# Joining the last layer norm with the shared expert and the router, and two scans in place of two loops

## What is computed

```python
x = x + _L0_xattn_ref(_layernorm(x), ...)      # cross attention
x = x + _L0_ffn_ref(_layernorm(x), ...)        # Hadamard-rotated FFN
x = x + _L1_xattn_ref(ctx, _layernorm(x), ...) # selective scan, gated by the norm of x
x = x + _L1_ffn_ref(_layernorm(x), ...)        # 16 experts, two per token, and a shared one

def _L1_ffn_ref(x, Wr, bias, Wg, Wu, Wd, sWg, sWu, sWd):
    xt = x.reshape(b * s, h)                   # 2048 tokens of 512
    probs = jax.nn.softmax(xt @ Wr.T + bias)   # 16 experts
    topk_val, topk_idx = jax.lax.top_k(probs, 2)
    w = topk_val / (jnp.sum(topk_val, axis=-1, keepdims=True) + 1e-9)
    ...                                        # y: each token through each expert
    routed = jnp.einsum('tke,tk,teh->th', one_hot(topk_idx, 16), w, y)
    shared = jax.nn.silu(xt @ sWg) * (xt @ sWu) @ sWd
    return (routed + shared).reshape(b, s, h)
```

## Time and profile before

| | us |
|---|---|
| median of 3 runs (2711.42 to 2715.6) | 2714.7 |
| profiled execution | 2715.96 |
| its span, first to last instruction | 2714.2 |
| last norm stage | 43.3 |

### The profile page before, as it was taken

How to read it: one execution, slowest core, us unless ns; L and a number is a source line. 1 busy time by engine, 2 the same in 40 slices (tenths; PEclk the granted TensorE clock), 3 DMA queues, 4 the chain that set the end, 5 groups by cost and what they waited for, 6 DMA issues and landing times. The chain is left out here.

```text
span 2714.2 us, 35174 instructions
## 1 busy us (share of the span) xinstructions
PE 2294.5 (85%) x10784; PEld 1768.1 (65%) x10785; DVE 1860.2 (69%) x3465; ACT 1229.2 (45%) x2129; POOL 1350.1 (50%) x1083
## 2 busy tenths in 40 slices
PE   3799999999999999997856997998988749468980
PEld 2688888888888888885525665665655427356770
DVE  6476777777676767765757999999989766312223
ACT  2354445445444545443655655656555312123430
POOL 0233333333333333331756778988888602577324
PEclk7799999999999999998977999999999958779995
DMA  7522232221223232112467564654554220755317
GB/s 280 218 75 79 86 110 86 109 87 72 82 86 110 86 110 85 63 67 81 139 219 216 177 205 144 213 175 172 180 195 156 61 90 16 250 164 183 120 54 259
DMA packets 136907, 363.57 MB, mean 134 GB/s; under 512 B 21281, under 2 KB 58913, under 8 KB 118561
## 3 DMA queue, kind: packets, MB, share of 16 engines
q1 hardware_dynamic: 123648, 328.36, 35.6%
q0 software_dynamic: 6320, 20.71, 2.4%
q10 hardware_dynamic: 6768, 12.32, 1.2%
HBM read 290.06 MB, written 71.30 MB: 133 GB/s over the span
## 5 line engine op out<-in xcount | busy, mean ns | idle before, releaser
L664 POOL TENSOR_SCALAR att_probs<-att_probs,att_recip 128x512 f32<-128x512 f32 x256 | 181.7, 713 | 563.1 <-DVE att_recip L731 563.1
L1809 POOL TENSOR_TENSOR mix_drive<-mix_du,mix_rows 128x512 f32<-128x512 f32 x256 | 326.6, 1282 | 63.2 <-DMA mix_rows<-bc_d 28.9
L588 ACT ACTIVATE att_probs<-att_s,att_bias,att_rq 128x512 f32<-128x512 f32 x256 | 200.4, 783 | 289.7 <-DVE att_bias L727 289.6
L1862 DVE TENSOR_TENSOR_SCAN mix_state<-mix_state,mix_drive 128x512 f32<-128x512 f32 x256 | 312.8, 1222 | 15.5 <-POOL mix_drive L1809 10.5
L1693 ACT ACTIVATE mix_state<-mix_delta,mix_a 128x512 f32<-128x512 f32 x256 | 176.7, 692 | 276.9 <-DVE mix_drive L1873 237.7
L1794 POOL TENSOR_TENSOR mix_y<-mix_y,mix_drive 128x512 f32<-128x512 f32 x180 | 230.4, 1280 | 78.2 <-DVE mix_drive L1873 78.2
L1602 PE MATMUL mix_down<-mix_wd,mix_hT 128*128 128x512 f32 x512 | 233.9, 600 | 7.5 <-DVE residual_x L1893 7.5
L726 DVE TENSOR_REDUCE att_nmax<-att_s 128x1 f32<-128x512 f32 x256 | 175.2, 684 | 71.7 <-PE att_s L101 64.8
L767 DVE TENSOR_TENSOR att_pT<-att_pt,att_pT 128x512 fp32r<-128x512 f32 x256 | 170.1, 686 | 65.0 <-ACT att_pT L594 61.3
L594 ACT CAST att_pT<-att_pt 128x512 fp32r<-128x512 f32 x256 | 144.0, 592 | 132.8 <-PE att_pt L445 128.5
L99 PE MATMUL att_w<-att_w_qkv,att_cx 128*128 128x256 f32 x512 | 158.6, 310 | 34.2 <-DVE att_w_qkv L713 25.5
(11 more groups left out here) (348 smaller groups left out, 6718.4 us busy)
## 6 DMA issues: line engine op xcount, KB each, us to landing
att_xn<-normT SPq DMA_DIRECT2D x32, 2048.0 KB
mix_gu<-guT SPq DMA_DIRECT2D x64, 1024.0 KB
mix_rows<-bc_d SPq DMA_DIRECT2D x128, 256.0 KB, 5.0
guT<-att_ffnT SPq DMA_DIRECT2D x32, 512.0 KB, 5.7
mix_wd<-wdT SPq DMA_DIRECT2D x16, 1024.0 KB
slots<-exp_y ACTq DMA_DIRECT2D x47, 256.0 KB
normT<-nrm_outT SPq DMA_DIRECT2D x4, 2048.0 KB, 9.3
exp_raw<-in_L_ffn_Wg SPq DMA_DIRECT2D x16, 512.0 KB
```

What stands on the lines that cost most here:

```text
L588: act.activation(probs[:, n, :], ps_s[n % 2][:, :], ACT.Exp, bias=bias[:, n:n + 1], scale=rq[:, n:n + 1], accum_out=sums[:, n:n + 1]).then ...
L664: pool.tensor_scalar(probs[:, n, :], probs[:, n, :], recip[:, n:n + 1], 1.0, ALU.mult, ALU.mult).then_inc(s_pn, 1)
L1809: pool.tensor_tensor(drive[q % RING][:, :], du[i % DUS][:, :], rows[g % ROWS][:, 0, :], ALU.mult).then_inc(s_drive, 1)
L1862: dve.tensor_tensor_scan(h[:, :], h[:, :], drive[q % RING][:, :], 0.0, ALU.mult, ALU.add).then_inc(s_scan, 1)
```

## The change

`stage_norm` keeps only its first use (the diff there takes out branches and is not shown). The last norm moves into the router's stage, now `stage_norm_router`, and is interleaved with the logits and batch 0's gate and up on each engine. The inverse root becomes one power on GpSimd. The transposes use the banks of `rou_y`, the logits the one bank `rou_bank`. TensorE waits at first for ident and wr alone. The two chains of additions become one scan each; for this `chosen`, `pre` and `place` are stored with the expert outside and the tile inside, and the mask `within` restarts the scan at every expert.

```diff
             def _(sp):
-                sp.dma_start(ident_sb[:, :], ident).then_inc(s_in, 16)
-                sp.dma_start(wr[:, :], Wr).then_inc(s_in, 16)
+                sp.dma_start(ident_sb[:, :], ident).then_inc(s_first, 16)
+                sp.dma_start(wr[:, :], Wr).then_inc(s_first, 16)
...
                 for b in range(B):
+                    sp.wait_ge(s_normed, TB * (b + 1))
+                    sp.dma_start(xrows[b * S:(b + 1) * S, :].rearrange("(t p) d -> p t d", p=P),
+                                 normed[b % 2][:, :, :]).then_inc(s_rowsout[b % 2], 16)
+                for b in range(B):
                     sp.wait_ge(s_yadd, TB * (b + 1))
...
             def _(pe):
+                def turn(b):
+                    for t in range(TB):
+                        pe.wait_ge(s_normed, TB * b + t + 1)
+                        if b:
+                            pe.wait_ge(s_lo, TB * (b - 1) + t + 1)
+                        for k in range(KD):
+                            tr = pe.transpose(ps_y[t][:, k * P:(k + 1) * P], normed[b % 2][:, t, k * P:(k + 1) * P],
+                                              ident_sb[:, :])
+                        tr.then_inc(s_tr, 1)
...
+                def route(b):
+                    pe.wait_ge(s_lo, TB * (b + 1))
+                    if b:
+                        pe.wait_ge(s_lcopied, b)
+                    for k in range(KD):
+                        mm = split_product(pe, bank[0:EXPERTS, :], (wrT[:, 0, k, :], wrT[:, 1, k, :]),
+                                           (xT[b][:, 0, k, :], xT[b][:, 1, k, :]), k == 0, k == KD - 1)
+                    mm.then_inc(s_l, 1)
...
-                pe.wait_ge(s_in, 16 * 6)
+                pe.wait_ge(s_first, 16 * 2)
...
+                turn(0)
                 pe.wait_ge(s_wlo, 1)
...
+                route(0)
+                turn(1)
+                gate(0)
+                up(0)
+                route(1)
+                turn(2)
+                gate(1)
+                turn(3)
+                route(2)
+                up(1)
+                route(3)
+                pe.wait_ge(s_lcopied, B)
+                for n in range(N):
+                    b, t = divmod(n, TB)
+                    tr = pe.transpose(ps_l[:, n, :], logitT[:, b, t * P:(t + 1) * P], ident_sb[0:EXPERTS, 0:EXPERTS])
                 tr.then_inc(s_lt, 1)
-                up_gate(0)
+                for j in range(IC, 2 * IC):
+                    gate(j)
+                    up(j)
+                pe.wait_ge(s_in, 16 * 4)
                 pe.wait_ge(s_chosen, 1)
                 pe.matmul(ps_c, ones[:, :], chosen[:, :, :], start=True, stop=True)
                 pe.matmul(ps_r, before_sb[:, :], chosen[:, :, :], start=True, stop=True).then_inc(s_counts, 1)
-                up_gate(1)
                 down(0)
...
             def _(act):
...
+                turned_hi(0)
+                for n in range(3):
+                    weights_hi(n)
+                logits_out(0)
+                turned_hi(1)
+                silu(0)
+                lift(0)
+                logits_out(1)
+                turned_hi(2)
+                silu(1)
+                turned_hi(3)
+                logits_out(2)
+                hi(0)
+                lift(1)
+                logits_out(3)
+                hi(1)
+                act.wait_ge(s_sub, 1)
+                act.activation(ex[:, :, :], logits[:, :, :], ACT.Exp).then_inc(s_ex, 1)
...
             def _(pool):
+                def invert(b):
+                    pool.wait_ge(s_var, b + 1)
+                    pool.tensor_tensor(rstd[:, b, :], var_eps[:, b, :], power[:, :], ALU.pow).then_inc(s_rstd, 1)
...
+                invert(0)
+                invert(1)
+                weights_lo(0)
+                weights_lo(1)
+                invert(2)
+                weights_lo(2)
+                invert(3)
...
             def _(dve):
+                norm_stats(0)
+                normalize(0)
                 dve.wait_ge(s_whi, 1)
                 dve.tensor_tensor(wrT[:, 1, :, :], ps_t, wrT[:, 0, :, :].bitcast(F32), ALU.subtract).then_inc(s_wlo, 1)
+                norm_stats(1)
+                turned_lo(0)
+                normalize(1)
+                norm_stats(2)
+                turned_lo(1)
+                normalize(2)
+                norm_stats(3)
+                turned_lo(2)
+                normalize(3)
...
+                turned_lo(3)
...
-                for n in range(N):
-                    own.after(dve.tensor_tensor(pre[:, n + 1, :], pre[:, n, :], pair[:, 0, n, :], ALU.add))
+                own.after(dve.tensor_tensor_scan(flat(pre), flat(within), flat(ps_c), 0.0, ALU.mult, ALU.add))
...
-                own.after(dve.tensor_copy(ends[:, 0:1], tiles[:, 0:1]))
-                for e in range(1, EXPERTS):
-                    own.after(dve.tensor_tensor(ends[:, e:e + 1], ends[:, e - 1:e], tiles[:, e:e + 1], ALU.add))
+                own.after(dve.tensor_tensor_scan(ends[:, :], ones[:, 0:EXPERTS], tiles[:, :], 0.0, ALU.mult, ALU.add))
...
-                own.after(dve.tensor_tensor(place[:, :, :], pre[:, 0:N, :], ps_r, ALU.add))
-                own.after(dve.tensor_tensor(place[:, :, :], place[:, :, :], repeat(first[:, :]), ALU.add))
+                own.after(dve.tensor_tensor(place[:, :, :], pre[:, :, :], ps_c, ALU.subtract))
+                own.after(dve.tensor_tensor(place[:, :, :], place[:, :, :], ps_r, ALU.add))
+                own.after(dve.tensor_tensor(place[:, :, :], place[:, :, :], spread(first[:, :], N), ALU.add))
```

More of the change, by code:

```diff
@@ L131, in stage_norm @@
         rstd = m.sb("rstd", [P, TB])
-        keep = isinstance(xT, list)
-        outT = xT if keep else [m.sb(f"outT{i}", [P, 2, KD, S], F32R) for i in range(2)]
+        outT = [m.sb(f"outT{i}", [P, 2, KD, S], F32R) for i in range(2)]
         banks = [m.ps(f"bank{t}", [P, KD, P]) for t in range(TB)]
@@ L2014, in stage_shared_router @@
         wr = m.sb("wr", [EXPERTS, DIM])
+        normed = [m.sb(f"normed{i}", [P, TB, DIM]) for i in range(2)]
+        xT = [m.sb(f"xT{b}", [P, 2, KD, S], F32R) for b in range(B)]
+        stats = m.sb("stats", [P, B, TB, 6])
+        meanvar = m.sb("meanvar", [P, B, TB, 2])
+        var_eps = m.sb("var_eps", [P, B, TB])
+        rstd = m.sb("rstd", [P, B, TB])
+        power = m.sb("power", [P, TB])
         wrT = m.sb("wrT", [P, 2, KD, EXPERTS], F32R)
@@ L2094, in _ @@
                                  xs[:, b * TB:(b + 1) * TB, :]).then_inc(s_st, 16)
+                for i in range(2):
+                    sp.wait_ge(s_rowsout[i], 16 * B // 2)
                 sp.wait_ge(s_st, 16 * B)
@@ new lines, in project @@
+                def project(j, which, out, done, free):
+                    b, ic = divmod(j, IC)
+                    cols = slice(ic * P, (ic + 1) * P)
+                    if j == 0:
+                        pe.wait_ge(s_sw, which + 1)
+                    if j:
+                        pe.wait_ge(free, j)
+                    for k in range(KD):
+                        mm = split_product(pe, out[:, :], (part(0, which, k)[:, cols], part(1, which, k)[:, cols]),
+                                           (xT[b][:, 0, k, :], xT[b][:, 1, k, :]), k == 0, k == KD - 1)
+                    mm.then_inc(done, 1)
@@ L2145, in _ @@
                 pe.matmul(ps_r, before_sb[:, :], chosen[:, :, :], start=True, stop=True).then_inc(s_counts, 1)
-                up_gate(1)
                 down(0)
-                up_gate(2)
+                for j in range(2 * IC, 3 * IC):
+                    gate(j)
+                    up(j)
                 for n in range(2 * N):
@@ L2153, in _ @@
                 down(1)
-                up_gate(3)
+                for j in range(3 * IC, 4 * IC):
+                    gate(j)
+                    up(j)
                 down(2)
@@ L2620, in build @@
                       du_d, bc_d, ident)
-        with Memory(nc, "normed2") as n:
-            normT2 = [n.sb(f"b{b}", [P, 2, KD, S], F32R) for b in range(B)]
-            stage_norm(nc, "nrm2", xs, normT2, ident, rowsout=xrows)
-            stage_shared_router(nc, xs, mixed, normT2, L1_ffn_sWg, L1_ffn_sWu, L1_ffn_sWd, L1_ffn_Wr, L1_ffn_bias, ident, iota, before, token, plan)
+        stage_norm_router(nc, xs, mixed, xrows, L1_ffn_sWg, L1_ffn_sWu, L1_ffn_sWd, L1_ffn_Wr, L1_ffn_bias, ident, iota,
+                          before, token, plan)
     stage_experts(nc, xrows, slots, L1_ffn_Wg, L1_ffn_Wu, L1_ffn_Wd, ident, plan)
```

197 lines of the change are left out of this document (99 added, 98 removed).

## The result

The changed kernel took 2678.6 us in the median of four executions (2675.9 to 2682.2), the kernel before 2713.65 (2711.4 to 2715.6): ratio 0.9872, 95% interval 0.9856 to 0.9888, 35.0 us less. (The ratios on record can differ by 0.001 from the quotient of the medians.) The prediction was 2683, range 2674 to 2701. The profiled execution took 2678.03 us, its span is 2676.2 against 2714.2. In a later run (e11) the same kernel had a ratio of 0.9868 (0.9853 to 0.9883).

A forecast was written before the change was run, and what follows sets the result against it. VectorE was taken to bound the last norm, TensorE the router stage from its first matmul; 21.4 us ahead of the router chain plus 10.9 behind made 32.3, 2715.96 to 2683.7 profiled, 2682.4 against the median; given 2683, range 2674 to 2701.

The forecast's parts named there:

- likeliest case: Whole kernel: a gain of 24 to 41 us, 2674 to 2691 us, chance 0.77; point gain 32.3 us.
- Inputs: Start of the joined stage: waiting for ident and wr alone removes 9.3 us and the boundary's 0.8 us.
- Power: Inverse root on GpSimd: 1.65 us plus 0.3 for hand-overs replaces 2.8; first normalization ends one us sooner.
- Clock: TensorE in the front: granted clock low through route(0), rising to full near +19, during turn(1).
- Hold by POOL: Second normalization in the front: GpSimd's work delays VectorE, costing 1.2 us through turn(3)'s wait.
- Behind the logits: After the router chain starts: batch 0's gate and up already done, batch 1's give cover; 10.9 us less.
- Scans: Counts to partf: 0.65 and 0.2 us; worth 0 against the old kernel, keeping 1.7 to 3 us in the new order.
- A: Front: clock stays low until the router begins, 12 us gain, 2703; with cases of 5 to 24 us gain, chance 0.16.
- B: Rest of the stage: TensorE stays at 1.2 GHz there too, 45 us slower, 2760; chance 0.03.
- C: Later stages or an unseen wait: the time comes back or was never there, within 0.2%; chance 0.04.

The follow-up runs named there:

- e11: Changed kernel run again, unaltered, against the kernel before: 2683.74 us, ratio 0.9868.
- e6: Kernel before, with TensorE waiting at the router stage's start for ident and wr alone: 2709.13 us, ratio 0.9978.
- e7: Changed kernel, with GpSimd's low weights held back until the second (gate, up) and third (down) normalizations are done: 2682.66 us, ratio 0.9894.
- e1: Kernel before, with only the two scans and the layout they need: 2712.69 us, ratio 1.0001.
- e3: Changed kernel, with the two chains of additions back in place of the scans: 2683.86 us, ratio 0.9903.
- e10: Changed kernel, with the Newton chain back on VectorE and GpSimd's low weights held until two, then three normalizations are done: 2694.87 us, ratio 0.9917.
- e5: Changed kernel, with the Newton chain back on VectorE in place of the power on GpSimd: 2694.80 us, ratio 0.9937.

## Why the prediction was right

The likeliest case gave 32.3 us; it was 35.3 in the stage and 35.0 in the medians, from the causes that the prediction names. By its steps:

- *Inputs.* Right: TensorE waits 3.98 us for wr, ahead of its first need. Alone the early wait is worth 6.7 us (e6), less than the 9.3 that stood between the first transfer and the first matmul, since 2.5 us of loading remain. (Of the six small transfers four, not all, were queued behind the large ones.)
- *Power.* 1.04 us, where I took 1.65 near the top of the range 0 to 1.73; normalization 0 began at +4.3 and not at +5.0, `route(0)` at +11.9 and not at +12.8.
- *Clock.* I let it rise near +19; it was full from about +15.5, near the end of `route(0)`, so this took 4.3 us and not 5.1, and `turn(1)` 1.9 and not 2.3.
- *Hold by POOL.* It was there (4.82 and 2.81 us), but I let it reach TensorE at `turn(3)` for 1.2 us. It reached nothing (e7). These three make the front 24.7 in place of 21.4 us: +43.0, not +46.3.
- *Behind the logits.* 10.6 for 10.9: gate and up of batch 1 cover the chain to `chosen` as batch 0's did. Logits to counts take 12.25 us, as before, and the held subtraction is back at 0.43 us. ScalarE loads its tables twice in this stretch, as before, and not once more as I had it. I didn't see the slower matmuls coming, 0.3 us a batch and 0.2 in `down(0)`. That only 0.3 us is missing in all is in part luck: batch 0's gate and up had taken 11.3 us and not 10.9, and `down(1)` took 7.7 for 8.0.
- *Scans.* 0.69 and 0.19 us for 0.65 and 0.2, and worth nothing in the old order (e1), as forecast. What they keep in the new order was mis-sized, 0.6 us at most (e3) for 1.7 to 3, because I read the old row of 5.03 us as the price of 15 additions, when 2.2 of it was a hold. It is no term of the sum. `chosen` stored across took 0.60 us, within the bound. VectorE waits 4.72 us at the fifth pair of tiles; I had 4.
- *Rivals.* A didn't happen in this kernel, but it did in e10, at one wait of 3.67 us; with the power TensorE has no wait for VectorE in the front behind the start of `route(0)`. The clock fell elsewhere too, in the kernel before as in the changed one: before, it was 0.50 from 2288 to 2300, among the source matmuls, behind waits of 0.27, 1.22 and 1.20 us for one-hot tiles. B fell: the clock is full up to the source matmuls, as before. Nothing showed in the stages behind (C): 384.4 us from the last add to the end for 386.1.

The sum was right, and the attribution less so. I gave the power 1 us; taking it back costs 12.4 in the new order, holds by POOL included, and putting it in is worth 6.3 to 8.6 in the old. I reckoned it on batch 0 alone and called the rest covered by VectorE's own work on the neighbouring batch. But with Newton it is VectorE that bounds the front (TensorE waits 12.5 and 1.9 us for it in e5, 6.2 and 3.7 in e10), so its freed 2.8 us per batch are the gain, and the forecast held them without naming them, in that the new order came out with TensorE as the bound.

## What to carry to other kernels

Cost an edit against the engine that bounds the stage after all the other edits, too: an operation moved off VectorE may look hidden in one batch and still be what lets TensorE run through. Before a row's duration is used as a price, look at what ran on GpSimd beside it. When a block of small matmuls waits for their operands one by one, put them a few at a time between large ones: here this was worth 10 us more, and it kept the clock up.

## What the runs showed of the hardware

- A power of 128x4 on GpSimd takes 1.01 to 1.04 us, and 1.73 for 128x8.
- A chain of small dependent VectorE instructions beside queued GpSimd instructions of 2.3 us was held at three links in a row: 2.20, 2.26 and 2.26 us for instructions of 0.16 (e5).
- After the matmuls of `route(0)` start, from 1.2 GHz, the granted clock of the same kernel was full in the second 4 us window of one trace and at 0.76 there in another, where the logits chain began 1.0 us later.
- The granted clock doesn't follow TensorE's work at once: 0.91 in four microseconds in which TensorE was busy for 0.72, then 0.57 under a full load (changed kernel, 2183 to 2191).
- The gate and up matmuls of 128x512 at full clock were 0.2267, 0.2288 to 0.2290 or 0.2333 to 0.234 us apart in kernels that differ in where buffers lie. 16 bytes a partition more ahead of the weights gave 0.2267 for 0.2333 (e5, e10). The cause is open.
